# A two-batch window attention: batch 1's projections as pieces between batch 0's jobs, norm roots on GpSimd, gathers with a limit on their lead

## What is computed

```python
q = (xp @ Wq + bq).reshape(B, Lp, H, D).transpose(0, 2, 1, 3)
k = (xp @ Wk + bk).reshape(B, Lp, G, D).transpose(0, 2, 1, 3)
v = (xp @ Wv + bv).reshape(B, Lp, G, D).transpose(0, 2, 1, 3)
...
scores = jnp.einsum('brgnqd,bgnkd->brgnqk', qg, kw) * scale
attn = jax.nn.softmax(scores, axis=-1)
og = jnp.einsum('brgnqk,bgnkd->brgnqd', attn, vw)
...
o = o[:, :L, :]
return o @ Wo + bo
```

## Time and profile before

| what | us |
|---|---|
| median of 3 runs (lowest, highest) | 1276.07 (1272.76, 1276.13) |
| the profiled execution, its own time | 1266.34 |
| its span, first to last instruction | 1264.6 |
| PE busy, share of the span | 1161.6 (92%) |
| DVE busy | 762.5 |
| ACT busy | 511.8 |
| POOL busy | 241.5 |
| mean granted clock of TensorE | 0.935 |

### The profile page before, as it was taken

How to read it: one execution, slowest core, us unless ns; L and a number is a source line. 1 busy time by engine, 2 the same in 40 slices (tenths; PEclk the granted TensorE clock), 3 DMA queues, 4 the chain that set the end, 5 groups by cost and what they waited for, 6 DMA issues and landing times. The chain is left out here.

```text
span 1264.6 us, 19609 instructions
## 1 busy us (share of the span) xinstructions
PE 1161.6 (92%) x6948; PEld 1014.3 (80%) x6948; DVE 762.5 (60%) x1588; ACT 511.8 (40%) x957; POOL 241.5 (19%) x271
## 2 busy tenths in 40 slices
PE   5999999999999999999999968599997489889996
PEld 5988899998988889998989856477766379768886
DVE  4756757566575656575665778444438654576644
ACT  5674443444343443434345552122213552353322
POOL 1111101011010101011110100233328222222211
PEclk9999999999999999999999978699988566889998
DMA  4001001000000000010000061333433240000001
GB/s 142 9 1 34 10 1 42 0 33 8 0 33 8 0 33 8 0 41 0 0 1 1 1 219 66 112 107 107 106 96 89 69 140 1 1 1 1 18 17 34
DMA packets 29289, 50.32 MB, mean 40 GB/s; under 512 B 5200, under 2 KB 19504, under 8 KB 27952
## 3 DMA queue, kind: packets, MB, share of 16 engines
q1 hardware_dynamic: 25136, 38.81, 9.2%
q0 software_dynamic: 4096, 10.75, 3.3%
HBM read 36.70 MB, written 10.49 MB: 37 GB/s over the span
## 5 line engine op out<-in xcount | busy, mean ns | idle before, releaser
L619 POOL TENSOR_TENSOR linear_out_squares<-linear_out_squares,lin_sq 128x512 f32<-128x512 f32 x64 | 91.2, 1426 | 599.8 <-ACT lin_sq L520 596.8
L41 PE MATMUL lin_bank<-keep_xT_hi,lin_w_hi 128*128 128x512 f32 x384 | 155.3, 404 | 2.6 <-DVE keep_xT_lo L230 2.6
L42 PE MATMUL lin_bank<-keep_xT_lo,lin_w_hi 128*128 128x512 f32 x384 | 152.4, 397 | 0.0
L43 PE MATMUL lin_bank<-keep_xT_hi,lin_w_lo 128*128 128x512 f32 x384 | 152.2, 396 | 0.0
L575 DVE TENSOR_TENSOR lin_st<-lin_bank,lin_mask 128x512 f32<-128x512 f32 x64 | 44.3, 692 | 175.7 <-PE lin_bank L430 175.7
L516 ACT ACTIVATE lin_o<-lin_bank 128x512 f32<-128x512 f32 x64 | 38.3, 599 | 191.4 <-PE lin_bank L461 191.4
L457 PE MATMUL lin_bank<-lin_st,lin_v 128*128 128x128 f32 x512 | 94.0, 275 | 0.0
L41 PEld LDWEIGHTS lin_bank<-keep_xT_hi,lin_w_hi 128*128 128x128 f32 x384 | 72.8, 190 | 17.9 <-issue 3.0
L461 PE MATMUL lin_bank<-lin_qd,lin_state 128*128 128x128 f32 x448 | 87.2, 276 | 0.0
L43 PEld LDWEIGHTS lin_bank<-keep_xT_hi,lin_w_lo 128*128 128x128 f32 x384 | 72.4, 189 | 17.7
L42 PEld LDWEIGHTS lin_bank<-keep_xT_lo,lin_w_hi 128*128 128x128 f32 x384 | 72.7, 189 | 14.7
(11 more groups left out here) (367 smaller groups left out, 2825.5 us busy)
## 6 DMA issues: line engine op xcount, KB each, us to landing
lin_raw<-in_wp SPq DMA_DIRECT2D x8, 1024.0 KB, 4.8
sorted_y<-linear_out_acc SPq DMA_DIRECT2D x48, 128.0 KB, 2.1
experts_up_expert_up<-in_wgu SPq DMA_DIRECT2D x16, 352.0 KB, 6.9
experts_down<-in_wdn SPq DMA_DIRECT2D x16, 176.0 KB
keep_x<-in_x SPq DMA_DIRECT2D x4, 512.0 KB, 7.5
lin_raw_out<-in_wop SPq DMA_DIRECT2D x8, 256.0 KB, 2.7
tokens_x<-linear_out_acc SPq DMA_DIRECT2D x4, 512.0 KB, 10.2
tail_q<-tail_qT SPq DMA_DIRECT2D x32, 64.0 KB, 2.0
```

The lines of the kernel that those rows point to most:

```text
L41: nc.tensor.matmul(out, lh, rh, start=first, stop=False, skip_group_check=skip)
L42: nc.tensor.matmul(out, lh, rl, start=False, stop=False, skip_group_check=skip)
L43: return nc.tensor.matmul(out, ll, rh, start=False, stop=last, skip_group_check=skip)
L619: pool.tensor_tensor(part, part, sq[:, a, :], ALU.add).then_inc(squares_sb, 1)
```

## The change

The norm's root is now made on POOL alone: `pool_scale` raises variance plus epsilon to the power -0.5 (an array of that exponent is set once), and ACT's roots and DVE's reciprocals go. Batch 1's first norm is applied by DVE (`dve_apply`). The zeroing of k2 and v2 goes from POOL, in the middle of the gathers, to DVE's start. Gathers of tile n wait until tile n-3 has arrived (`AHEAD`). Jobs run with rr inside mq. Batch 1's turn, its k and v projection, its two q pieces and its turn of v stand in PE's iterations 1, 3, 4, 5 and 6, with the matching pieces on ACT and DVE; the weighing and norms of `c0` and `c1` are in the loop too. Banks are given out anew (one for values, one for output products), k is moved by SP's queue, and ACT copies v and half of the q rearrangements.

```diff
-    def dve_spread(self, dve, chain, k):
+    def dve_known(self, dve, chain, k):
         chain.wait()
         for i in range(self.n):
-            chain.step(dve.bn_aggr(self.mean_var[k][:, i, :], self.stats[k][:, i, :]))
-        chain.wait()
-        dve.tensor_scalar(self.spread[k][:], self.mean_var[k][:, :, 1], LN_EPS, None, ALU.add).then_inc(self.spread_ready[k], 1)
...
+            dve.bn_aggr(self.mean_var[k][:, i, :], self.stats[k][:, i, :]).then_inc(self.known[k], 1)
+
+    def pool_scale(self, pool, chain, k):
+        pool.wait_ge(self.known[k], self.n)
+        chain.step(pool.tensor_scalar(self.minus[k][:], self.mean_var[k][:, :, 0], -1.0, None, ALU.mult))
+        chain.link(pool.tensor_scalar(self.spread[k][:], self.mean_var[k][:, :, 1], LN_EPS, None, ALU.add))
+        chain.link(pool.tensor_tensor(self.scale[k][:], self.spread[k][:], self.power[:, 0:self.n], ALU.pow))
+        pool.tensor_tensor(self.shift[k][:], self.minus[k][:], self.scale[k][:], ALU.mult).then_inc(self.affine_ready[k], 1)
...
+    def dve_apply(self, dve, k):
+        dve.wait_ge(self.affine_ready[k], 1)
+        for i, t in enumerate(self.tiles):
+            last = dve.tensor_scalar(self.part(k, i), self.source(k)[:, t, :], self.mean_var[k][:, i, 0:1], self.scale[k][:, i:i + 1],
+                                     ALU.subtract, ALU.mult)
...
-        RING = 8
+        RING, AHEAD = 8, 3
...
-        o = [spare[:, x, :] for x in range(2)]
+        o = [sb(f"o{x}", [P, 4 * 2 * GD])[:] for x in range(2)]
...
-        JOBS = [(b, rr, mq) for b in range(BATCH) for rr in range(RR) for mq in range(4)]
-        NJ = len(JOBS)
+        JOBS = [(b, rr, mq) for b in range(BATCH) for mq in range(4) for rr in range(RR)]
+        NJ, NB = len(JOBS), len(JOBS) // BATCH
+        kv_bank, q_bank, v_bank, tail_bank = (bank[0:2], turned), (bank[2:4], turned), (bank[5], bank[7]), (bank[2], bank[5])
...
+                    if n >= AHEAD:
+                        pool.wait_ge(arrived[ORDER[n - AHEAD]], 2 * DMA)
...
+                    if n == 6:
+                        a.pool_scale(pool, chain, "y")
+                    if n == 9:
+                        a.pool_scale(pool, chain, "x")
+                    if n == 12:
+                        b.pool_scale(pool, chain, "y")
+                b.pool_scale(pool, chain, "x")
+                c0.pool_scale(pool, chain, "y")
...
+                dve.memset(k2[:], 0.0).then_inc(k_zero, 1)
+                dve.memset(v2[:], 0.0).then_inc(v_zero, 1)
...
+                net.dve_step(dve, chain, *STEPS[5])
+                weigh(b, 1, 2, 3)
+                a.dve_low(dve, turned)
+                a.dve_low_tail(dve, tail_bank[0])
+                weigh(b, 4)
+                b.dve_known(dve, chain, "y")
+                dve.wait_ge(a.added, a.adds())
+                b.dve_apply(dve, "y")
+                b.dve_x(dve, chain)
+                arrange(0)
...
+                b.act_apply(act, "x")
+                values(0)
+                arrange(1)
                 for i in range(NJ + 4):
+                    if i == 2:
+                        b.act_high(act, turned)
+                        b.act_high_tail(act, tail_bank[1])
+                    if i == 4:
+                        take_kv(1)
+                    if i in (5, 6):
+                        take_q(1, i - 5)
+                    if i == 5:
+                        duplicate(1)
+                    if i == 7:
+                        values(1)
...
-                        if n >= 2:
-                            pe.wait_ge(raw_o_sb, n - 1)
+                        if n >= 1:
+                            pe.wait_ge(raw_o_sb, n)
...
+                    if i == 1:
+                        pe.wait_ge(used[0].low, KT + 1)
+                        used[1].pe_turn(pe, turned)
+                        pe.wait_ge(v_sb, 1)
+                        used[1].pe_turn_tail(pe, tail_bank[1])
+                    if i == 3:
+                        project_kv(1)
+                    if i in (4, 5):
+                        project_q(1, i - 4)
+                    if i == 6:
+                        turn_v(1)
```

322 lines of the change are left out of this document (153 added, 169 removed).

## The result

The changed kernel took 1246.35 us in the median of 4 runs (1245.21 to 1247.87), the kernel before 1275.04 on the same chip (4 runs, 1272.76 to 1276.13): 28.7 us less, a ratio of 0.9778 with a 95% interval of 0.9759 to 0.9797. The forecast was 1250.6 in a range of 1237 to 1268.

The account below looks back on a forecast made before the run. PE was taken to bound the jobs at both clocks. Head, loop and drain put the stage's end at 1083.8 to 1084.0 against 1109.5, 25.5 us earlier: 1240.8 profiled, plus 9.7 to the median, 1250.6 us; range 1237 to 1268.

Parts of the forecast that it names:

- Up to turn 10: Tail stage: batch 0's turn at 979.7, first projection 984.6, second job's scores 1007.0, turn 10's scores 1047.5.
- The step on the clock: Job loop: PE's granted clock high from about 1021, with one fall around the waits for ACT, 2.3 us.
- the wait for q: Job loop: the tenth job waits until ACT has copied batch 1's moved q, at 1041.9.
- The 1.2 us of the lock: End of the head: DVE's copy of q and POOL's last scale wait each other out, 1.2 us added.
- The eager add and statistics of segment 0: Late loop: 3.5 us on DVE in one iteration, 2 of them on PE's path, giving 1081.5.
- the one bank of the values' and output products: Loop: one bank for values, one for output products; waits for ACT's or DVE's reading cost nothing unless ACT is late.
- The offset to the median: Final sum: before's median lay 9.7 us above its profile; the same difference added to 1240.8 gives 1250.6.
- The wait on arrivals at nothing: POOL's gathers: tile n asks for tile n-3, issued 5 us earlier and landing in 2.7 (4.1 at most); no cost.
- The zeroing at nothing: DVE's start: zeroing takes about 4.5 us, covered by 7.79 us of idle time; no cost, 4.5 at worst.
- The clock that rises only with the first output product: Rival on the loop's clock: stage ends 1090.9, 18.6 us earlier, 1257.5 us; chance 0.20.
- The late q: Rival: batch 1's 16 q moves at 1.39 us put the tenth job 11.4 us later; 1262 us, chance 0.08.
- the slow case: Rival: the clock never rises in the loop; stage ends 1122.8, 13.3 us later, 1289.4 us, chance 0.07.

Follow-up runs that it names:

- the spread variant: Changed kernel with the first norm's add and the next norm's two statistics halves spread over turns 13, 14, 15, ACT's apply one turn earlier: 1238.42 us, ratio 0.9794.
- The one variant that would have told the cast's form apart: Kernel before with DVE's cast to the high part written as a maximum of h with itself: 1263.49 us against 1264.01, ratio 0.9996.

## Why the prediction was right, and where it was wrong

**The direction and the three large causes: right.** The head got shorter (turn of batch 0 and first projection within 1 us of the forecast), batch 1's chain went between the jobs, and the clock was high through most of the loop. The experiments show that the parts need each other: the order alone gives 1.5 us, the norms alone 5.3, the zeroing alone loses 3.9, and the order taken out of the changed kernel costs 11 to 13. Batch 1's pieces between the jobs, the largest part of the edit, were never tested by themselves, so what they bring is argued from the trace and not shown.

**Up to turn 10: the number right to 1.6 us, by another path.** Forecast 979.7, 984.6, 1007.0 and 1047.5, measured 980.63, 985.58, 1008.20 and 1049.06. The step on the clock, high from about 1021 with one fall, is what happened: the first row of a projection at the higher clock is at 1021.63. But the sum books the 2.3 us of the fall behind turn 10, at its end, and comes to 1047.5 by way of the wait for q. The copy of q was done at 1042.00, as forecast (1041.9), and PE did not wait for it: it worked without a gap from 1034.56 on, 7 us of that at the low clock, and reached turn 9's scores at 1044.60 only. In one execution of the variant without the wait on arrivals the fall didn't come at all, though PE had the same small gap of 0.25 us ahead of it. PE there:

```profile
1033.72 1.94 PE L2241 MATMUL tail_bank<-window_wo,tail_oP 128*128 128x256 f32 x8
...
1039.20 1.16 PE L2195 MATMUL tail_bank<-tail_k,tail_q 64*128 64x128 f32 x8 [0.63 <-ACT tail_q L2070]
```

The first output product takes 1.94 us and turn 9's scores do wait for q, 0.63 us. Turn 10 began 105.0 us after the first gather, against 106.0 to 106.9 in five executions with the fall. So the fall cost 1.0 to 1.9 us on the path, since q would have held PE back anyway; fall and wait were priced as a sum and stand beside each other. Why the fall came in all but one execution isn't shown. The 1.2 us of the lock, too, are in 1007.0 and once more in 1047.5; the working doesn't show that the 1041.9 between them was reckoned without it.

**The collision on the shared port: right, a little smaller.** I had added 1.2 us for DVE's copy of q beside POOL's scale. DVE's timeline in the changed kernel:

```profile
999.20 1.26 DVE L1955 COPY tail_q<-tail_q 64x2048 f32<-64x2048 f32 x1 [2.15 <-DMA tail_q<-tail_qT]
```

and POOL's:

```profile
999.12 0.26 POOL L1702 TENSOR_SCALAR tail_used_minus_x<-tail_used_mean_var_x 128x5 f32<-128x5 f32 x1
999.46 1.10 POOL L1703 TENSOR_SCALAR tail_used_spread_x<-tail_used_mean_var_x 128x5 f32<-128x5 f32 x1
```

The second small operation took 1.10 us where it takes 0.25 elsewhere: 0.85 us. DVE's five applies (1.59 us for four, from 991.24) stood beside gathers of 0.95 to 1.12 us, durations that gathers have without them as well (1.12 at 955.10). The Trainium skill ("SBUF — State Buffer", Who interferes with whom) has the lock, and counts tensor_scalar among the operations that can take it, when its operands meet the conditions of the two-port mode. For the copy the trace agrees; tensor_scalar of this form, at 0.40 us for 256 columns, held up nothing that the trace shows.

**The end of the stage: this term was mis-sized.** I forecast 1083.8 to 1084.0, measured 1088.6 (the last row of statistics). The step that failed reads "The eager add and statistics of segment 0 put 3.5 us on DVE in one iteration; I take 2 of them on PE's path". They came to 4.5, as the spread variant measured. The path took 2.15 as a gap, near what I had taken, and then the clock fell to 0.57 for 8 us, which I had not priced. A second, smaller part is the one bank of the values' and output products, where the forecast said "I cost it at nothing": 1.5 us in the loop's second half and the drain; pairs took 6.98 us and not 6.71. From turn 10 to the end of the stage it was 39.5 us against 34.0 in the sum (20.1, 5.4, 6.5 and the 2): 2.5 of the 5.5 too few are the stall, 1.5 the banks, and 1.5 stay unassigned, most of them in the drain.

**The offset to the median: wrong, and it covered the error before it.** My sum for the profiled execution was 1240.8, against 1245.69 measured: 4.9 too low. I then added 9.7 us, the distance of before's profile to its median, as if it belonged to chip and run: "the same difference there gives 1250.6". It didn't; the changed kernel's profile is 0.7 us off its median. The 9.7 were, as far as the traces tell, the hold during POOL's gathers, which the profiled execution of before didn't have and all profiled variants beside a before of 1274 did. So 25.5 forecast and 28.7 measured between the medians is luck in part, two errors of opposite sign: 4.9 us too much gain in the sum, and 8.1 us that the profiles don't have and the medians do, the hold for the most part.

**The wait on arrivals at nothing: right.** In the kernel before it doesn't break the row of gathers, and the changed kernel with and without it lies within the intervals. **The zeroing at nothing: no sign against it in the changed kernel** (DVE's first product came 4.2 us after the first gather, 4.6 before), **wrong as a part by itself**: without it POOL's row in the kernel before is 22 gathers long, and in the one trace of it ACT comes back 31.0 us after the first gather, against 28.2 with the new order.

**The rivals.** The clock that rises only with the first output product was half right: it was high before it, fell in all but one execution, and then rose only with it. The late q did not happen (16 moves in 10.0 us, no gap ahead of turn 9 with the fall and 0.63 us without), and the slow case, the clock never rising, is out.

**What stays open** is what the hold is. Three engines with nothing in common but POOL's gathers stand still, PE between two products of one row, and it goes with the chip, as far as five chips at most show. The lock on the port would explain DVE alone; by the Trainium skill ("SBUF — State Buffer", Terms) PE and ACT have ports of their own, and both stood still. The Trainium skill ("Runtime: NRT & Kernel Launch", Instruction fetch mechanics) says that each engine loads its own instructions over a DMA queue while it runs; instructions that wait behind gathers could look like this. No run here shows it, and the one sign that the traces hold speaks against it: they record packets of two instruction queues, and in the variant with the zeroing moved none comes between 947 and 996, while ACT stood still from 951 to 972. Which engines these queues serve isn't shown. The one variant that would have told the cast's form apart ran on a chip without a hold.

## What to carry to other kernels

Before the distance between a profile and the median is carried over to a forecast, look for an idle time in the one that the other may not have; a variant's profile beside it shows it soonest. Look at long unbroken rows of indirect gathers on GpSimd: in seven of these traces another engine stood still until about the row's end, and the kernel with work between its gathers lost less by it, though no run shortened the row alone. Price a gap of TensorE at the high clock twice, once as itself and once as what the clock costs behind it; here 2.15 us became 4.5. And where a low clock and a wait for another engine cover the same time, take the longer of the two and not the sum.

## What the runs showed of the hardware

- On three of five occasions engines stood still during 14 to 22 gathers issued in a row (ACT idle for up to 20.7 us at a time, DVE for 13.8, single products of PE 1.0 us apart) and came back 2 to 3.5 us after the last; the same program took 1264 to 1265 or 1274 to 1275 us from chip to chip.
- Where TensorE's granted clock was low in the loop, it rose beside the first block of 256-column output products, and the scores behind that block ran at the high clock: 1066 to 1068 in the earlier trace rows, 1068.67, 1049.95 and 1038.32 in the kernels above. The projections raised it earlier, and in all but one execution it fell again between. It fell once more behind the gap in the drain: to 0.57 behind 2.15 us in the changed kernel; without that gap it stayed at 1.00.
- The power on GpSimd took 1.21 to 1.34 us for 5 columns and 0.88 for 3 (1.04 for 4 in the earlier trace rows); a whole scale of 5 columns from aggregates to shift 2.3 us.
- Of the 21.0 us between the two profiled executions 16.3 are the same products at a higher granted clock, 0.81 instead of 0.70 over the stage.
